# Scatters of 128 partitions instead of 125 into the sorted edge tables of a four-layer graph network

## What is computed

```python
edge_index = jnp.stack([src, dst])
x = _layernorm(x + _L0_gnn_ref(x, edge_index, W, b, a, 3125))          # sums by src
x = _layernorm(x + _L1_gnn_ref(x, edge_weight, ..., edge_index))       # softmax by dst
x = _layernorm(x + _L2_gnn_ref(x, edge_index, ...))                    # two attention layers, by dst
x = _layernorm(x + _L3_gnn_ref(x, weight, gamma, beta, src, dst, edge_type_8))  # by dst
```

## The kernel before

| stage | what the other engines do | scatters |
|---|---|---|
| bucket (L330) | DVE finds the slot of each edge by `src` | none |
| dst_in (in `sort_edges`, L438) | DVE loads and casts the edges for the sort by `dst`, fills `stage_all` | 12, src |
| hist | DVE and PE count keys | 46, src |
| rank | DVE ranks each edge within its key, 85 groups of 5 columns | 176, src |
| proj0 (`project`) | products for the first layer, rows stored by SP | 46, src |
| srcblend (`blend`) | last 92 columns of src, on DVE, ACT and PE | 53, src |
| up0 (`attend_update`) | end of the first layer, norm on DVE | 25, dst |
| proj1 (`project`) | products for the second layer, rows stored by SP | 45, dst |
| dstblend (`blend`) | last 192 columns of dst | 163, dst |

## Time and profile before

### The profile page before, as it was taken

One profiled execution on the slowest core, in us unless ns is written; L12 is line 12 of the kernel. 1 busy time (PEld: TensorE's weight loads), 2 busy tenths in 40 slices (PEclk: granted clock), 3 DMA queues, 4 the chain that ended last, 5 costly groups with the idle time before them and its releaser, 6 DMA issues. The chain is left out here.

```text
span 5221.9 us, 60063 instructions
## 1 busy us (share of the span) xinstructions
PE 3871.0 (74%) x16731; PEld 2963.9 (57%) x16731; DVE 3452.2 (66%) x6698; ACT 1886.0 (36%) x3980; POOL 3018.5 (58%) x3023
## 2 busy tenths in 40 slices
PE   0666667776498788876788887988888799855553
PEld 0566356665144666663566666866666576544443
DVE  8998845555687666667689986659999743222224
ACT  0000622221386333325466663436666443200001
POOL 2686767776777767740466762127777321077772
PEclk9755866666699777777899998999999899977776
DMA  1133144444201544452677873137777611233334
GB/s 49 44 97 81 25 123 133 133 131 82 60 3 21 142 128 129 130 90 94 186 220 222 236 213 97 42 102 233 227 226 228 169 64 71 111 105 105 106 105 67
DMA packets 281736, 630.51 MB, mean 121 GB/s; under 512 B 71564, under 2 KB 126192, under 8 KB 278256
## 3 DMA queue, kind: packets, MB, share of 16 engines
q0 software_dynamic: 159168, 436.21, 32.6%
q1 hardware_dynamic: 122288, 190.89, 11.2%
HBM read 560.35 MB, written 65.91 MB: 120 GB/s over the span
## 5 line engine op out<-in xcount | busy, mean ns | idle before, releaser
L1020 PE MATMUL edge_sums<-edge_rows,edge_hot 128*128 128x272 f32 (+2 forms) x3712 | 1251.5, 503 | 589.7 <-issue 249.3
L1020 PEld LDWEIGHTS edge_sums<-edge_rows,edge_hot 128*128 128x128 f32 x3712 | 919.0, 256 | 848.6 <-issue 498.1
L953 POOL DMA_INDIRECT edge_rows<-kv_rows,dst_index x928 | 877.6, 946 | 625.5 <-issue 258.6
L1030 DVE TENSOR_TENSOR l_acc<-l_acc,edge_sums 128x272 f32 (+2 forms) x928 | 394.7, 425 | 468.0 <-PE edge_sums L1020 448.6
L953 POOL DMA_INDIRECT edge_rows<-rel_rows,dst_other_index x464 | 438.7, 945 | 234.3 <-issue 138.0
L953 POOL DMA_INDIRECT begun_rows<-xl_rows,dst_index x464 | 443.2, 955 | 192.1 <-issue 134.9
L953 POOL DMA_INDIRECT edge_rows<-rows,src_index x464 | 438.6, 945 | 164.3 <-issue 131.3
L208 POOL DMA_INDIRECT table_src<-src_src_stage_all x333 | 415.5, 1248 | 155.0 <-issue 100.0
L1284 PE MATMUL edge_own_rows<-dst_x,edge_hot_t 128*128 x1856 | 464.0, 395 | 30.2 <-ACT edge_hot_t L984 20.4
L1284 PEld LDWEIGHTS edge_own_rows<-dst_x,edge_hot_t 128*128 128x128 f32 x1856 | 354.2, 196 | 92.4 <-issue 35.6
L1030 DVE TENSOR_TENSOR last_acc<-last_acc,edge_sums 128x256 f32 x232 | 97.7, 421 | 428.7 <-PE edge_sums L1020 428.4
(11 more groups left out here) (454 smaller groups left out, 6934.2 us busy)
## 6 DMA issues: line engine op xcount, KB each, us to landing
edge_where<-local_dst SPq DMA_DIRECT2D x174, 256.0 KB, 3.9
dst_rank_keys<-in_dst SPq DMA_DIRECT2D x85, 312.5 KB, 3.3
rel_rows<-nodes_out SPq DMA_DIRECT2D x25, 1024.0 KB, 3.8
edge_where<-local_src SPq DMA_DIRECT2D x58, 256.0 KB, 3.5
edge_rows<-kv_rows,dst_index POOLq DMA_INDIRECT x928, 3.9
kv_rows<-nodes_out SPq DMA_DIRECT2D x50, 260.0 KB, 2.0
edge_rows<-rows,src_index POOLq DMA_INDIRECT x464, 2.8
begun_rows<-xl_rows,dst_index POOLq DMA_INDIRECT x464, 2.9
```

The costliest lines, as they stand in the source:

```text
L953: pool.indirect_dma_start(out=self.rows[:, h * U + b, 0:self.width], out_offset=None, in_=self.source[:, :], in_offset=bass.IndirectOffset ...
L1020: last = nc.tensor.matmul(sums[p % len(sums)][:, 0:width], self.hot[s % 2][:, 2 * (p % 4) + i, :], self.half(s)[:, 2 * (p % 4) + i, first: ...
L1030: nc.vector.tensor_tensor(into, into, sums[p % len(sums)][:, 0:width], ALU.add).then_inc(stored, 1)
```

## The change

A scatter takes all 128 partitions of `stage_all`. Partitions 125 to 127 have no edges. Their target rows come from a new constant `beyond`, which numbers rows behind the table: 3 x 425 = 1275 spare rows are added to each table, and each column has three of its own. What they carry is zero. The clearing and the later reads of the tables leave the spare rows out.

```diff
+SPARE = P - EP
+TABLE = P * PT + SPARE * ET
...
+    k.beyond = hold.sb("beyond", [P, ET], i32)
...
             nc.gpsimd.memset(k.ones[:, :], 1.0)
+            nc.gpsimd.iota(k.beyond[:, :], pattern=[[SPARE, ET]], base=P * PT - EP, channel_multiplier=1)
...
-        self.stage_all = hold.sb(f"{tag}_stage_all", [EP, ET, 5], i32)
+        self.stage_all = hold.sb(f"{tag}_stage_all", [P, ET, 5], i32)
...
-            mine = scatter.stage_all[:, first:ET, :]
+            mine = scatter.stage_all[0:EP, first:ET, :]
...
-                sp.dma_start(table.rearrange("(p t) w -> p t w", p=P)[:, half * PT // 2:(half + 1) * PT // 2, :],
+                sp.dma_start(table[0:P * PT, :].rearrange("(p t) w -> p t w", p=P)[:, half * PT // 2:(half + 1) * PT // 2, :],
...
             step(nc.vector.memset(stage_all[:, :, :], 0))
+            step(nc.vector.tensor_copy(stage_all[:, :, 0], k.beyond[:, :]))
...
                 step(nc.vector.memset(stage_all[:, :, :], 0))
-                nc.vector.tensor_copy(stage_all[:, 0:ET, 1], cols[1][:, :])
-                nc.vector.tensor_copy(stage_all[:, 0:ET, 3], key_c[:, :])
+                step(nc.vector.tensor_copy(stage_all[:, :, 0], k.beyond[:, :]))
+                nc.vector.tensor_copy(stage_all[0:EP, 0:ET, 1], cols[1][:, :])
+                nc.vector.tensor_copy(stage_all[0:EP, 0:ET, 3], key_c[:, :])
...
-                by_dst = Scatter(front, "dst", scratch("table_dst", (P * PT, 4), i32), 192, 3)
+                by_dst = Scatter(front, "dst", scratch("table_dst", (TABLE, 4), i32), 192, 3)
...
-                    by_src = Scatter(near, "src", scratch("table_src", (P * PT, 4), i32), 92, 2)
+                    by_src = Scatter(near, "src", scratch("table_src", (TABLE, 4), i32), 92, 2)
```

More of the change, by code:

```diff
@@ L405, in _ @@
             nc.vector.tensor_tensor(rows[:, :], lead[:, 1:NT + 1], lead[:, 0:NT], ALU.subtract).then_inc(counted, 1)
-            nc.vector.tensor_copy(stage_all[:, 0:ET, 1], other_i[:, :])
-            nc.vector.tensor_copy(stage_all[:, 0:ET, 3], key_i[:, :])
+            nc.vector.tensor_copy(stage_all[0:EP, 0:ET, 1], other_i[:, :])
+            nc.vector.tensor_copy(stage_all[0:EP, 0:ET, 3], key_i[:, :])
             dve.wait_ge(summed, 1)
@@ L430, in _ @@
             step(nc.vector.tensor_scalar(tile_i[:, :], slot_i[:, :], 7, None, ALU.arith_shift_right))
-            nc.vector.scalar_tensor_tensor(stage_all[:, 0:ET, 0], in_tile[:, :], float(PT), tile_i[:, :], ALU.mult, ALU.add)
+            nc.vector.scalar_tensor_tensor(stage_all[0:EP, 0:ET, 0], in_tile[:, :], float(PT), tile_i[:, :], ALU.mult, ALU.add)
             scatter.keep(nc, in_tile, tile_i)
@@ L484, in _ @@
                 sp.wait_ge(blank, 3)
-                sp.dma_start(table.rearrange("(p t) w -> p t w", p=P), empty[:, :, :]).then_inc(wiped, 16)
+                sp.dma_start(table[0:P * PT, :].rearrange("(p t) w -> p t w", p=P), empty[:, :, :]).then_inc(wiped, 16)
                 sp.wait_ge(wiped, 16)
@@ L524, in _ @@
                                                         ALU.mult, ALU.add))
-                    nc.vector.tensor_copy(stage_all[:, 0:ET, 2], relation[:, :])
-                    nc.vector.tensor_copy(stage_all[:, 0:ET, 4].bitcast(fp32), cols[3][:, :])
+                    nc.vector.tensor_copy(stage_all[0:EP, 0:ET, 2], relation[:, :])
+                    nc.vector.tensor_copy(stage_all[0:EP, 0:ET, 4].bitcast(fp32), cols[3][:, :])
             @block.tensor
@@ L712, in finish @@
                     step(nc.vector.tensor_scalar(mine(slot_i), mine(slot_i), 7, None, ALU.arith_shift_right))
-                    nc.vector.scalar_tensor_tensor(stage_all[:, bass.ds(i * SLOTS * LOOK, SLOTS * LOOK), 0], mine(in_tile),
+                    nc.vector.scalar_tensor_tensor(stage_all[0:EP, bass.ds(i * SLOTS * LOOK, SLOTS * LOOK), 0], mine(in_tile),
                                                    float(PT), mine(slot_i), ALU.mult, ALU.add).then_inc(finished, 1)
@@ L828, in _ @@
         def _(sp):
-            sp.dma_start(raw[:, :, :], table.rearrange("(p t) w -> p t w", p=P)).then_inc(loaded, 16)
+            sp.dma_start(raw[:, :, :], table[0:P * PT, :].rearrange("(p t) w -> p t w", p=P)).then_inc(loaded, 16)
             sp.wait_ge(rowed, 1)
```

## The result

| | us |
|---|---|
| before, four runs | 5228.99, 5228.91, 5222.87, 5220.83, median 5225.89 |
| after, four runs | 5175.19, 5177.12, 5171.28, 5161.67, median 5173.23 |
| ratio | 0.9906, 95% interval 0.9885 to 0.9927 |
| profiled execution of after: its time, its span | 5175.19, 5173.4 |

The change makes the kernel faster by 0.94%.

What follows compares the result with a forecast made beforehand. POOL's scatters were taken to bound six stages by their barriers and to slow DVE in rank. Barriers 22.1 plus rank 15 made 37.1 us, taking 5228.9 to 5192 us, with a range of 5177 to 5215.

Steps and rivals of the forecast that it cites:

- the term for rank: In rank, scatters shut DVE's L688 out for part of their length; shorter ones gain 15 us, ends 0 and 18.7.
- proj1: Stage whose barrier waits 4.3 us for POOL: gain 4.1 us, then SyncE's last store is last.
- up0: Stage where POOL stays last: 18 scatters shorter by 0.242 us give 4.4 us; ceiling 9.7 if one more passes ahead.
- The scatter: One scatter instruction on POOL: from 1187 ns to about 945, the time of a 128-row gather.
- The barriers that are given back whole: Stages where POOL's saving exceeds its lateness at the barrier: gains dstblend 8.7, srcblend 2.9, proj0 0.7 us.
- dst_in: Stage whose barrier waits 2.2 us for POOL; less hand-over and new copy on DVE's path, gain 1.3 us.
- in step at its worst: Case for rank: four of five L688 still delayed some 0.15 us each, 9.7 us left, gain 9.0 us.
- at random: Case for rank: L688 meets the shortened shut window by chance, 1.3 us left over 81 executions, gain 17.4 us.
- The small edits: Iota, bucket copy, memset, extra writes and hist: all come to 0, with 1 us as bound.
- the cost by rows: Rival: a scatter grows to 1215 ns, kernel about 5240 us, chance 0.07; staying at 1187 gives 5229, chance 0.11.
- barriers without rank: Rival: L688 keeps its 712 ns, only the barriers' 22.1 us come, 5207 us; chance 0.20.
- a change that does nothing: Rival: source still taken as 125 partitions, 5229 us; within the chance for no difference, 0.11.

Runs made afterwards that it cites:

- e4: The kernel after without the 176 scatters of rank, their edges left out of the first table: rank 265.03 us, whole time 5182.41 us.
- e6: The kernel after timed again with no edit, against the kernel before: median 5179.49 us over 6 runs, ratio 0.9904.
- e1: The kernel after with other row counts per scatter (64 to 128) by stage, only scatter durations read: median 910 ns at 64 rows, 1392 at 123.
- e2: The kernel after with 125 rows per scatter again in every stage but rank, which keeps 128: 5201.32 us, ratio 0.9961 to the kernel before.
- e3: The kernel after with 125 rows per scatter again in rank alone: 5197.2 us, ratio 0.9955 to the kernel before.
- e5: The kernel after with columns of both tables shared out anew, fewer placed by matrices and more by scatters: 5139.91 us, ratio 0.9827 to the kernel before.

## Why the prediction was wrong, and where it was right

**The step that failed** is the term for rank. "I take 15 [...] with 0 and 18.7 as the ends" priced one instruction of DVE, L688, and halved between two cases; the stage gave 20.1 to 20.7 us, above the stated end, and e4 puts all that scatters cost the stage before at 21.2. Two smaller terms were short by the same kind of error, something left at nothing: the DMA queues in proj1 (4.1 for 5.5) and one more scatter ahead of the block in up0 (4.4 for 5.5). The mechanism named for the barriers and for rank was right. That the first four runs have their median below the range and the six of e6 have theirs inside it is the spread of the runs.

**The scatter.** 945 was forecast with 1215 as the other bound; it is 958. The 945 was taken over from a gather with the same row count, and no run ties the two, so that it came so near is in part luck. The reason given, that fewer bytes of filling have to be laid out, was in the right direction. e1 makes it precise: what counts is the rows in each group, 8 for 25, since all 16 packets have as many entries as that. One support for it was read wrongly: the 32 packets of a scatter against the 48 of a gather are no mark of 125 rows, since a scatter of 128 rows makes 32 packets too. What tells them apart is the size of the packets.

**The barriers that are given back whole.** dstblend 8.7 forecast and 8.1 measured, srcblend 2.9 and 2.7, proj0 0.7 and 0.4. POOL's saving was several times the excess in each, and the other engine named ends the stage now. Reading the excess at the barrier was enough.

**proj1**, 4.1 forecast, 5.5 measured. The excess was right, but SyncE itself arrives 1.4 us earlier (66.9 us into the stage for 68.3). ACT's wait for stores to land, `DMA res_rows<-proj_out`, fell from 3.9 to 1.1 us in the groups of the stage, and scatters land in 2.1 us for 2.7. The step that failed here is the one on the queues: under 9% busy, so nothing comes of them. That share was read in dstblend; in proj1 the scatters had 9.8% beside 32.3% for SyncE's stores, and they have 2.7% now. I had asked only whether more packets could hurt, not whether less time in them could help. The difference repeats: SyncE arrives 67.7 to 68.3 us into the stage in the four profiles with 123 or 125 rows there, and 66.0 to 67.4 in the eight with 128. That it comes through the DMA engines is argued from the waits; no run tried it alone.

**dst_in**, 1.3 forecast, 1.9 measured. The new copy costs its 0.58 us, but three casts of the stage became shorter, from 0.80 to 0.56, from 0.64 to 0.55 and from 0.84 to 0.55, 0.6 us together; the last two had each begun 0.9 us into a scatter and do not now. So DVE is through 33.3 us into the stage as before, and only the hand-over, now 0.3 us, is left of the 2.2.

**up0**, 4.4 forecast, 5.5 measured. The mechanism is the one given, 18 scatters times the saving; one more passed ahead of DVE's long instructions, as the ceiling had it, and its period of 1.26 us is the difference.

**Rank**, 15 forecast, 20.1 to 20.7 measured. This is the term that was mis-sized most, and its ceiling of 18.7 was too low. Two errors. First I took a middle between two cases, in step at its worst (9.0) and at random (17.4), and L688 came out beyond the better one. The shut part is still there, about 0.25 us long, as these two lines of the timeline of rank show, against the earlier trace rows:

```profile
246.13 0.96 POOL L212 DMA_INDIRECT table_src<-src_src_stage_all  x1 [0.30 <-issue]
246.65 0.73 DVE L694 TENSOR_SCALAR dst_rank_low_i<-dst_rank_keys 128x625 int32<-128x625 int32 x1 [0.39 <-issue]
```

It starts 0.51 us into the scatter and ends 0.285 after its end, as before.

But only 3 of the 85 fall in it. At random it would be some 17 (0.25 of 1.26 us). The two engines still run in step: 37 of the starts lie 0.15 to 0.27 us into a scatter and 19 at 0.74 to 0.86, on both sides of the shut part. That this step is a good one is luck, though little hangs on it: at random the delays would be an estimated 2.1 us in all (17 of 0.125), and they are 0.7. Second, I priced L688 alone. Over the whole stage it gives 18.2 us (59.6 to 41.4), the tensor_scalar behind it in the loop 1.3 more (562 to 547 ns over 85). DVE's wait for its keys, `DMA dst_rank_keys<-in_dst`, gives the other 0.6 (3.9 to 3.3). The floor of e4 is 21.2 us below before, and that is the ceiling that the term should have had. e2 and e3 show that rank's part is a matter of its own scatters alone.

**The small edits** stayed under the 1 us that was their bound: hist is 0.15 us longer, bucket 0.2, and the stage with the iota ahead of the first barrier 0.3 (4.46 to 4.73), which I had put at nothing.

**The sum** of the stages was 37.1 forecast and is 43.5 to 44.0. 6.4 to 6.9 are missing and rank has 5.1 to 5.7 of them; the other terms are 2.0 short together, and small stages between are some 0.7 longer. All three rivals fell: the cost by rows with e1, barriers without rank with e2, and a change that does nothing with the 958 ns of the scatter.

**The absolute number.** Two things outside the sum made the miss larger. I kept 7.0 us between the span and the median of the runs as if it belonged to the kernel. In every later execution with both numbers the distance is 1.7 to 1.9 us (5175.19 to 5173.4), so the profiled execution of before took an estimated 5223.7; the 7.0 held more of the runs' spread than of the kernel. And I took 6 us as the spread of runs, from three; before spread over 33 us (5206 to 5239) in 20 runs beside e1 to e4, with a median of 5221.8. 43.5 us off 5226 is 5182, inside the range of 5177 to 5215. That the first four runs of after have 5173 is most likely this spread: the code without scatters goes up and down by some 40 us in the profiles, one of its passes alone by 30. The mean granted clock of an execution moves with its time: of the 32 runs of before beside the experiments the fastest, 5205.59, has 0.826 and the slowest, 5249.02, has 0.816. Which passes get the clock and why is open; nothing was tried on it. A range with this spread would have begun near 5170.

## What to carry to other kernels

A scatter that GpSimd issues for many small rows should have a row count with a large divisor up to 16: the instruction took 24% longer with 125 rows than with 128, and 37% longer with 124, so spare rows that write behind the table are cheaper than leaving partitions out. When an engine's unit of work becomes cheaper, what it gives at barriers is soon used up; deal out the shares again, which here gave 35 us more, 34 of them in the two blend stages, beside the 43.5 of the change itself (e5). And read what an engine costs its neighbour as a term of the same rank as its own lateness: nearly half of this gain, 20 of 43.5 us, was VectorE's.

## What the runs showed of the hardware that was not expected

- A GpSimd scatter of 16-byte rows costs 13 ns for each row in a group and 840 to 860 ns besides (e1), but for two counts: 124 rows lie 50 ns above that, and 120 rows in 15 groups of 8 are slower (983 ns) than 128 in 16 groups of 8 (958).
- Groups that have no rows are still filled: with 125 rows 11 packets of 100 bytes go out for nothing, and with 124 rows 12 of 124 bytes.
- A scatter holds back a short DVE instruction only in a part of its own length. Before, L688 ran late when it started 0.55 to 0.80 us into a scatter of 1187 ns, and on time up to 0.53 and again at 0.99; after, late at 0.51 to 0.65 into one of 958 ns, and on time up to 0.27 and from 0.74. Each late one of both kernels ended 0.283 to 0.288 us behind the end of the scatter. The Trainium skill, SBUF — State Buffer, section "Who interferes with whom", says of DVE in its two-port modes and GpSimd that whichever issues first gets the shared pair of ports "for the whole instruction". A scatter as the first of the two does not agree, since it lets L688 through in its first half microsecond. Where a long DVE instruction is first it looks like that rule: four scatters of each kernel last 6.5 to 12.2 us, and one of before that starts 1.3 us into DVE's 6.8 us ends 1 us behind it.
- POOL's drain behind scatters became longer in most stages when they became shorter: 5.6 us for 1.9 in dstblend, 3.7 for 2.1 in proj1, and 2.1 as before in up0. It lay in time that POOL had to spare; at the end of rank in e5, with 8.6 us, it no longer did. What it works off there was not tried.
